# Sixteen tiles' P rows fetched ahead of the Q table, and seven more kept in DRAM, in a one-core graph-network layer

## The reference

```python
h = relu(layernorm(x))
feat = concat([h[src], h[dst]], axis=1)            # one row per edge, 2048 wide
e = relu(feat[kind] @ W_kind + b_kind)             # kinds by edge number: 256 hh, 1280 oo, 7168 ho
logit = (e @ W_a + b_a)[:, 0]
ex = exp(logit - segment_max(logit, dst)[dst])
alpha = ex / segment_sum(ex, dst)[dst]
z = segment_sum(alpha[:, None] * h[src], dst)      # attention over the edges of each node
out = x + relu(concat([h, z], axis=1) @ W_node + b_node)   # W_hn for nodes 0 to 127, W_on for the rest
```

## Time and the profile before

| what | value |
|---|---|
| median of 3 runs | 462.35 us (462.26 to 465.7) |
| the profiled execution: its time, its span | 462.58 us, 460.7 us |
| TensorE busy | 413.8 us, 90% of the span |
| VectorE busy | 326.3 us, 71% |
| GpSimd busy | 246.1 us, 53% |
| ScalarE busy | 146.8 us, 32% |
| mean granted TensorE clock | 0.963 |
| bytes moved by DMA | 116.02 MB, mean 252 GB/s |

### The profile page before, as it was taken

How to read it: one execution, slowest core, us unless ns; L and a number is a source line. 1 busy time by engine, 2 the same in 40 slices (tenths; PEclk the granted TensorE clock), 3 DMA queues, 4 the chain that set the end, 5 groups by cost and what they waited for, 6 DMA issues and landing times.

```text
span 460.7 us, 4728 instructions
## 1 busy us (share of the span) xinstructions
PE 413.8 (90%) x1622; PEld 287.8 (62%) x1628; DVE 326.3 (71%) x614; ACT 146.8 (32%) x216; POOL 246.1 (53%) x213
## 2 busy tenths in 40 slices
PE   1899999999999999999999999999999992019996
PEld 1688888886868888854444444675788881004844
DVE  5790463202999849996977997679999778995423
ACT  3841111413131335657464411213241104322100
POOL 2032007204577877777887777777888876300000
PEclk9999999999999999999999999999999997557999
DMA  8999868956654787879757576887788899392111
GB/s 312 383 322 425 342 232 285 411 203 254 268 190 147 217 301 244 279 221 328 241 191 228 197 234 199 321 275 276 282 285 280 273 370 321 103 357 94 46 70 68
DMA packets 40440, 116.02 MB, mean 252 GB/s; under 512 B 13609, under 2 KB 13609, under 8 KB 34656
## 3 DMA queue, kind: packets, MB, share of 16 engines
q1 hardware_dynamic: 14384, 64.07, 37.6%
q0 software_dynamic: 21760, 43.26, 28.7%
q10 hardware_dynamic: 4272, 8.39, 4.7%
HBM read 125.93 MB, written 17.86 MB: 312 GB/s over the span
## 4 chain that ended last, share of the span: by engine, by line
PE 28%; DVE 20%; issue 17%; POOL 17%; DMA 16%; ACT 1%; POOLq 0%; DVEq 0%
PE bank L884 6%; PE bank L886 6%; PE bank L885 6%; POOL gath L1159 6%; POOL gath L1152 6%; DMA pairs_ho<-logit,cell 6%; DVE gath L620 5%; DMA gath<-q_ho,q_index 5%; PE bank L1098 3%; POOL pairs_ho_odd L1171 3%; DVE gath L623 2%; POOL pairs_ho L1171 2%; PE bank L1073 2%; DMA gath<-q_oo,q_index 2%; DVE g_raw L561 2%
## 5 line engine op out<-in xcount | busy, mean ns | idle before, releaser
L884 PE MATMUL bank<-w_hi,h_t 128*128 128x512 f32 x368 | 145.9, 396 | 0.3 <-DVE h_t L568 0.3
L886 PE MATMUL bank<-w_hi,h_t 128*128 128x512 f32 x368 | 143.4, 390 | 0.0
L885 PE MATMUL bank<-g_raw,h_t 128*128 128x512 f32 x368 | 143.4, 390 | 0.0
L620 DVE TENSOR_TENSOR gath<-gath 128x512 f32<-128x512 f32 x118 | 76.1, 686 | 46.1 <-DMA gath<-q_ho,q_index 36.5
L1159 POOL DMA_INDIRECT gath<-q_ho,q_index x56 | 67.7, 1209 | 41.3 <-DMA q_ho<-stage 24.5
L325 ACT ACTIVATE w_hi<-raw 128x1024 fp32r<-128x1024 f32 x48 | 48.3, 1059 | 118.6 <-PE bank L886 56.4
L561 DVE TENSOR_TENSOR g_raw<-raw,w_hi 128x512 fp32r<-128x512 f32 x96 | 60.1, 688 | 31.2 <-ACT w_hi L325 31.2
L884 PEld LDWEIGHTS bank<-w_hi,h_t 128*128 128x128 f32 x368 | 69.1, 188 | 18.2 <-issue 4.4
L1152 POOL DMA_INDIRECT gath<-p_ho,i_src x49 | 55.2, 1126 | 46.5 <-DMA p_ho<-stage 31.8
L886 PEld LDWEIGHTS bank<-w_hi,h_t 128*128 128x128 f32 x368 | 69.1, 188 | 14.4
L885 PEld LDWEIGHTS bank<-g_raw,h_t 128*128 128x128 f32 x368 | 69.1, 188 | 14.1 <-issue 0.5
(11 more groups left out here) (144 smaller groups left out, 360.8 us busy)
## 6 DMA issues: line engine op xcount, KB each, us to landing
raw<-w_chunks SPq DMA_DIRECT2D x40, 1024.0 KB, 6.0
gath<-x SPq DMA_DIRECT2D x4, 512.0 KB, 5.1
h_dram<-h_sb SPq DMA_DIRECT2D x1, 2048.0 KB, 12.7
p_ho<-stage ACTq DMA_DIRECT2D x2, 1024.0 KB, 4.9
p_oo<-stage ACTq DMA_DIRECT2D x2, 1024.0 KB, 7.7
q_oo<-stage ACTq DMA_DIRECT2D x2, 1024.0 KB, 9.5
h_again<-h_dram SPq DMA_DIRECT2D x1, 2048.0 KB, 10.7
x_again<-x SPq DMA_DIRECT2D x2, 1024.0 KB, 8.9
```

The costliest lines, as they stand in the source:

```text
L620: i = nc.vector.tensor_tensor(p[:, cols], p[:, cols], q[:, cols], ALU.add)
L884: nc.tensor.matmul(to, hi, w_high, start=first, stop=False)
L885: nc.tensor.matmul(to, hi, w_low, start=False, stop=False)
L886: return nc.tensor.matmul(to, lo, w_high, start=False, stop=last)
```

## The change

- **AHEAD** grows from 7 to 11 tiles (5 to 15). The four further homes are three new buffers (`early_rows`) and `bias[:, 0]`. The room in SBUF comes from `dynamic_dma_scratch_size=4096`, where the default is 16384 bytes per partition.
- **KEPT**: the P rows of tiles 16 to 22 are gathered first of all, into the seven old homes; SyncE stores each in DRAM (`kept_rows`) before its load of chunk 9. When all seven stores have landed, GpSimd gathers the rows of tiles 5 to 11 into those homes. SyncE reads the kept rows back into the slots, five before its load of chunk 16 and two before that of chunk 17. GpSimd's loop then issues P rows from tile 23 on, where it did from tile 12 on.
- The sum `h_block` moves out of VectorE's early part into the tiles, since its place is a P buffer now. The order of tiles, splits and one-hots on VectorE is another.
- ScalarE exponentiates the ho and hh tables before it evacuates the second G half; VectorE weighs them block by block, between the late maxima and the attention of the first blocks; TensorE's first transpose waits for the first G remainder alone.

```diff
-AHEAD = tuple(range(SLOTS, SLOTS + 7))
+AHEAD = tuple(range(SLOTS, SLOTS + 11))
+KEPT = tuple(range(max(AHEAD) + 1, max(AHEAD) + 8))
+KEPT_AT = {16: 5, 17: 2}
...
+        early_rows = sb("early_rows", [P, 3, D], f32)
+        early_p += [*(early_rows[:, a] for a in range(3)), bias[:, 0]]
...
+            def kept_p_rows(n):
+                sp.wait_ge(s_logit, done_before(n))
+                sp.dma_start(edge_p[:, SLOT_OF[n]], kept_rows[KEPT.index(n)]).then_inc(s_krow[SLOT_OF[n]], 16)
+
+            kept = iter(KEPT)
             for c in range(RAW, PH_Z):
+                if c == 9:
+                    for i in range(len(KEPT)):
+                        sp.wait_ge(s_early[i], 16)
+                        sp.dma_start(kept_rows[i], early_p[i]).then_inc(s_kept, 16)
+                for _ in range(KEPT_AT.get(c, 0)):
+                    kept_p_rows(next(kept))
                 load(c)
...
             g_hi(0)
+            act.wait_ge(s_peak, 1)
+            for b in ORDER:
+                for kind in (0, 2):
+                    nc.scalar.activation(tab_sb[kind][:, b], tab_sb[kind][:, b], ACT.Exp, bias=peak[:, 4, b:b + 1]
+                                         ).then_inc(s_exp, 1)
             g_hi(1)
-            exps(0, 1, 4)
-            exps(2, 1, 4)
...
             split_lo(9)
-            tiles(3)
             split_lo(10)
-            tiles(3)
+            tiles(9)
             split_lo(11)
             tiles(3)
             split_lo(12)
             tiles(4)
             split_lo(13)
+            tiles(2)
+            sum_h_block()
+            tiles(1)
+            split_lo(14)
             tiles(4)
...
-            g_lo(0)
-            tiles(2)
             peak_ho()
             tiles(3)
+            g_lo(0)
+            tiles(1)
             g_lo(1)
-            weigh_exps()
+            weigh_exps(0)
+            weigh_exps(1)
...
+            late_peak(ORDER[0])
+            weigh_exps(2)
+            attention(0)
+            late_peak(ORDER[1])
+            weigh_exps(3)
+            attention(1)
...
-            pe.wait_ge(s_glo, 2)
+            pe.wait_ge(s_glo, 1)
             transpose_att(0)
...
+            for home, n in enumerate(KEPT):
+                early_p_rows(n, home)
             for n in range(SLOTS):
                 p_rows(n)
...
+            for home in range(len(KEPT), len(AHEAD)):
+                early_p_rows(AHEAD[home], home)
+            pool.wait_ge(s_kept, 16 * len(KEPT))
+            for home in range(len(KEPT)):
+                early_p_rows(AHEAD[home], home)
             pool.wait_ge(s_qst, Q_STORES[2])
...
-                    if n not in AHEAD:
+                    if n not in AHEAD and n not in KEPT:
                         p_rows(n)
...
-    nc = bacc.Bacc("TRN2", target_bir_lowering=False, num_devices=1)
+    nc = bacc.Bacc("TRN2", target_bir_lowering=False, num_devices=1, dynamic_dma_scratch_size=4096)
```

More of the change, by code:

```diff
@@ L85, with kept_visit @@
 VISIT = [SLOT_OF[:n].count(SLOT_OF[n]) for n in range(T_NODE)]
-P_VISIT = [sum(SLOT_OF[m] == SLOT_OF[n] and m not in AHEAD for m in range(n)) for n in range(T_NODE)]
+P_VISIT = [sum(SLOT_OF[m] == SLOT_OF[n] and m not in AHEAD + KEPT for m in range(n)) for n in range(T_NODE)]
+def kept_visit(n):
+    return sum(SLOT_OF[m] == SLOT_OF[n] for m in KEPT[:KEPT.index(n)])
 def done_before(n):
@@ L216, in build @@
         s_early = [sem(f"early_p_rows_landed{n}") for n in AHEAD]
+        s_kept = sem("p_rows_kept")
+        s_krow = [sem(f"kept_p_rows_landed{i}") for i in range(SLOTS)]
         s_esum, s_logit = sem("edge_summed"), sem("logit_ready")
@@ L768, in _ @@
             split_lo(13)
+            tiles(2)
+            sum_h_block()
+            tiles(1)
+            split_lo(14)
             tiles(4)
-            split_lo(14)
-            tiles(1)
             split_lo(15)
-            tiles(2)
[L774 to L779, removed]
+            tiles(4)
             one_hots(2)
             tiles(1)
[L782 to L790, removed]
+            for n in range(10):
+                one_hots(3)
                 tiles(1)
@@ L794, in _ @@
             tiles(2)
+            unpack_part(1)
+            tiles(1)
             one_hots(1)
-            unpack_part(1)
-            tiles(2)
-            one_hots(1)
+            tiles(1)
             weigh_hh(0)
-            tiles(2)
+            tiles(1)
             split_lo(25)
             tiles(4)
+            weigh_hh(1)
+            tiles(1)
             split_lo(27)
             tiles(1)
-            weigh_hh(1)
+            unpack_part(2)
             tiles(2)
             split_lo(29)
-            tiles(1)
-            unpack_part(2)
-            tiles(1)
+            unpack_part(3)
+            tiles(2)
             split_lo(31)
@@ L814, in _ @@
             tiles(2)
-            unpack_part(3)
-            tiles(1)
             split_lo(33)
@@ L851, in lower_att, with attention @@
                                         ).then_inc(s_atlo, 1)
-            for n, b in enumerate(ORDER):
+            def attention(n):
+                b = ORDER[n]
                 dve.wait_ge(s_exp, 2 * NB + 2 * n + 2)
                 step(nc.vector.tensor_tensor(tab_sb[1][:, b], tab_sb[1][:, b], counts[:, 1, b], ALU.mult))
+                dve.wait_ge(s_wexp, n + 1)
                 nc.vector.scalar_tensor_tensor(out=att[:, b], in0=tab_sb[0][:, b], scalar=drop_exp[:, b:b + 1],
@@ L1110, in _ @@
             pe.wait_ge(s_atlo, 1)
+            pe.wait_ge(s_glo, 2)
             combine(0, 0)
```

61 lines of the change are left out of this document (29 added, 32 removed).

## The result

The changed kernel takes 472.0 us (median of 4 runs, 470.58 to 472.65) against 464.02 us for the kernel before, timed beside it (4 runs). The ratio is 1.0159, with a 95% interval of 1.0087 to 1.0232: it is slower by 0.9 to 2.3%, where 454 was forecast. The profiled execution took 471.38 us with a span of 469.6; that of before 462.58 and 460.7.

The account below looks back on a forecast made before the run. The prediction took GpSimd's tiles to bound the kernel before 412 us, with TensorE setting the end after the change. First attention 8.5 us earlier, 3.7 from shorter weighing, the rest from earlier tiles: 462.6 - 8.5 = 454, range 447 to 464.

Parts of the forecast that it names:

- late first tile: VectorE's first tile: added transfers in full DMA queues were to move its start from 115.6 to 127.3 us.
- TensorE's stop for chunk 11: Near 143 us: chunk 11's split stands behind nine tiles on VectorE, so TensorE was to stop for 8.1 us.
- the sum of 22.5 MB: Bytes counted before the first tile can start: 56.3 us at 400 GB/s from 71 us, giving 127.3.
- the one-hots: First one-hot rows behind tile 26: 83.4 us after the start, 7.0 us late, held to lie inside the 8.1 already lost.
- the odd table: Load of the odd oo table near the end: to land at 397.1, before VectorE asks at 398.8, so no cost.
- GpSimd's loop alone: GpSimd's 54 turns, 4.54 us each, were taken to hold the tiles; eleven P gathers fewer were to free 15.7 us.
- the far bound (132.7): Latest bound for the first tile's start: 132.7 us, at 365 GB/s, the full-share rate of a stretch with many scattered reads.
- Turns of 3.0 us up to tile 22: GpSimd's 18 turns without P: 3.0 us each, reaching tile 23 58.2 us after the first tile starts.
- the rival: Shorter descriptor area makes each GpSimd DMA issue dearer; at 0.1 us each the time is 469. Chance 0.1.
- Chunk 9's load: SyncE's load behind the kept stores: some 5 us later than at 83, at no cost since ScalarE wants it at 102.
- The end: From G done at 390.6: evacuation 2.1, remainder 2.4, weighing through attention 8.8, so first attention at 403.9 instead of 412.4.
- The rival with the longer backlog: First tile starts at 131 to 137 us; each microsecond costs one, time 458 to 464, no measurable change. Chance 0.22.

Follow-up runs that it names:

- the run with chunk 9 first: Changed kernel with SyncE's load of chunk 9 ahead of the seven kept stores instead of behind them: 471.75 us, ratio 1.0209.
- the kernel with free rows: Changed kernel without kept tiles, splits in old order, upper_att(0) ahead of late_exps(1), and P rows of tiles 16 to 22 not fetched: 454.48 us, ratio 0.9769.
- the first experiment: Changed kernel without the seven kept tiles: eleven tiles gathered ahead, nothing stored or read back: 462.07 us, ratio 0.9971.

## Why the prediction was wrong

The path was named rightly (late first tile, TensorE's stop for chunk 11, first attention), but three of its terms failed. The first attention was forecast at 403.9 and ended at 421.1. Of the 17.2 us between them, 5.9 are the start of the first tile: the sum of 22.5 MB was too small. A further 6.0 are the price of the stop, put at its bare length: the clock behind it, and the one-hots that were held to lie inside it. And 3.5 are the end, almost all of it the wait of 3.2 us for the odd table, put at nothing. 1.8 are left, of which 0.7 stood already before the stop. The bytes alone would have made it 460 by the prediction's own sum (454 + 5.9); the other two took it past 464.

**What bounds the kernel before.** That the tiles end its chain was read rightly: the last tile ends at 397.5 and G at 382.5, and with the splits in their place and no kept rows, the shorter loop and the new end bring 6.0 us together (458.47 against 464.4). That GpSimd's loop alone sets them was not: with eleven P gathers out of it for nothing, tile 24 leads by 11.5 us and the last Q rows by 5.0.

**The transfers.** The queues moved 24.35 MB where the sum had 22.5; I had left out a further weight chunk (1.05 MB) and Q rows behind those of the first tile (0.7). At the measured 393 GB/s that is 62.0 us from 71, hence 133 and not 127.3. Of the 5.9 us some 4.7 are bytes, 1.0 the rate, and 0.2 rounding. The rate of 400 was nearly right; the page's rule of 358 GB/s ("DMA: Bandwidth & Descriptors", section "Specifications", in the Trainium skill) gave 134 by luck, by two errors that cancel: a rate too low here and my sum too small. The first tile was at the far bound (132.7) and just past it. The second wave of gathers was issued from 104.02 to 112.7 and not by 103, but the run with chunk 9 first shows that this is not what held the tile.

**The stall.** The mechanism was right, at the place named: 13.97 us at 143 us, where the same formula with the start of 133.2 gives 14.0. What failed is that it was priced at its length. The granted clock stood at 0.50 when TensorE came back: in the rows above, 2.59 busy us at 0.50 and 4.00 at 0.79 lose 1.3 + 0.8 = 2.1 us. The one-hots stopped TensorE once more, 2.2 us, where I had put their 7.0 us inside the first stop; behind it the clock was 0.83 for 10 us, 1.7 more. By the prediction's sum, 83.4 us after a start of 133.2, the first one-hot would come at 216.6, ahead of TensorE's 221.20; the turns that took longer (next paragraph) are the likely reason for the wait. 0.7 us are older than the stop: ScalarE's split at 85.85 before comes at 86.51. That leaves 1.1 us that I can't place. 0.7 + 14.0 + 2.1 + 2.2 + 1.7 + 1.1 = 21.8, which is 404.32 - 382.56 for G. I had 8.1.

**Turns of 3.0 us up to tile 22.** They took 3.35 us even in the kernel with free rows, and in the changed kernel GpSimd reached tile 23 65.0 us after the first tile, not 58.2. The kernel before already shows it. Its turns 5 to 11 have no P rows either; they begin with this line and end at 142.88, 3.27 us a turn:

```profile
119.96 1.55 POOL L1159 DMA_INDIRECT gath<-q_ho,q_index  x1 [0.31 <-issue]
```

The issues were not dearer by the descriptor area, as the rival had it (ratio 1.0012), but the mean of the earlier trace rows is no fixed price: see below.

**Chunk 9's load** went out 10 us later (93.42), not 5, because each store is issued when its rows have landed. ScalarE waited 7.2 us for it. That it costs nothing was right all the same (471.75).

**The end.** From G to the first attention it took 16.8 us, not 13.3. The odd table was late: SyncE issues `h_again`, 2 MB that wait for TensorE, ahead of it. With TensorE so late both loads went out together and the table took 8.9 us instead of the 4.4 of the earlier trace rows. I had called the tables not binding from the tiles alone, and not followed SyncE's queue. Moved, the wait goes and the time is 468.04.

Together: 403.9 + (21.8 - 8.1) + (16.8 - 13.3) = 421.1. The rival with the longer backlog named the right start but priced a microsecond of delay at one; it cost more. Without the kept tiles and with the splits in the old order the change is a gain, which the runs show. That the kept tiles don't pay here is shown too: for nothing they bring some 3 us, and their bytes delay the first tile by up to 16.7 us. Two things stay open: the 1.1 us, and what eats the lead behind tile 24.

## What to carry to other kernels

Before a transfer is moved into a stretch where the DMA engines are full, count every queue's bytes up to the moment that counts, the prefetches of other engines too, and divide by the stretch's own rate; what fits is nearly free, and what doesn't is paid (here 3.15 MB cost 4.6 us, the next 4.19 MB 12.1). Where an engine's order is fixed, a late input delays whatever stands behind it, so a long run of optional work ahead of something that another engine waits for makes every slip a stall. A stop of TensorE can cost more than its length: after the 14.0 us here another 2.1 went to the lower clock. And where a price is taken from a mean over the whole run, look first for rows of the same kind of turn: here the 3.27 us stood in the trace of before.

## What the runs showed of the hardware

GpSimd's indirect DMAs cost more in the mean while VectorE is busy. In the timelines of the kernel before, from 60 us on, those in whose time VectorE was busy for under 5% took 0.98 us in the mean, none of 30 over 1.3; those with VectorE busy for over 95% took 1.23, and 56 of 144 were over 1.3. In the changed kernel it is 0.97 (33, none) and 1.22 (146, 57). It holds late in the run as well (from 140 us, before: 0.99 and 1.23). It is no matter of the DMA engines' load alone: the 23 P gathers ahead of the Q rows in the changed kernel, issued while these are full, took 0.93 to 1.23 us. So a gather moved from the loop to a stretch with an idle VectorE was cheap here. The cause is not shown, and VectorE's busy share isn't all of it: with half of the addition left out, VectorE was busy for 62.28 of 70 us instead of 68.56 and GpSimd's 42 instructions took no less (53.64 us against 53.15). The Trainium skill ("SBUF — State Buffer", section "Who interferes with whom") tells of a pair of ports that VectorE and GpSimd share under an exclusive lock, and says that a VectorE instruction with two inputs from SBUF gets in the way only of GpSimd instructions that read SBUF; whether that is what is seen here no run shows.

Around the end of a stop of 4.5 us (the first experiment) the granted clock was 0.60 from 192 to 196 us and 0.55 in the next four. During the one of 14.0 us it fell to 0.51 and 0.50, the lower of its two levels (1.2 of 2.4 GHz), stayed there to 160 us, 2.6 us after TensorE's restart, and was 1.00 again from 164 us.
